# Batch 2's first-layer weights fetched ahead of layer 0's adapters, and those adapters handled behind layer A of batch 1

## The reference

```python
# layer 0
c0 = einsum('bsi,boi->bso', x, L0_cond_weight[ids0])          # one of 8 weights per batch: "W0 of batch b"
y  = einsum('bsd,od->bso', c0, L0_ffn_weight) + bias          # "W1"
lo = (c0 @ A[adapter].T) @ B[adapter].T                       # layer 0's adapters, rank 16, some batches without
x  = x + y + lo
# layer 1
c1 = x @ W2.T + b2 + scale[ids1] * ((x @ a[ids1].T) @ b[ids1].T)   # layer 1's adapters, rank 16
H  = c1 @ W3.T + b3
z  = c1 @ A3                                                  # rank 32
# softmax gates over 8 experts from H[:, odd tokens, :8] and z, scaled by their global maxima
x  = x + (H + (z * p_mix) @ Bmat * scaling)
```

## Time and profile before

| what | us |
|---|---|
| median of three runs | 122.72 (122.25 to 123.53) |
| the profiled execution | 123.07 |
| its span on the core | 121.3 |
| TensorE busy in it | 115.5 |
| VectorE, ScalarE, GpSimd busy | 84.4, 58.4, 24.0 |

### The profile page before, as it was taken

How to read it: one execution, slowest core, us unless ns; L and a number is a source line. 1 busy time by engine, 2 the same in 40 slices (tenths; PEclk the granted TensorE clock), 3 DMA queues, 4 the chain that set the end, 5 groups by cost and what they waited for, 6 DMA issues and landing times.

```text
span 121.3 us, 1920 instructions
## 1 busy us (share of the span) xinstructions
PE 115.5 (95%) x694; PEld 98.1 (81%) x694; DVE 84.4 (70%) x177; ACT 58.4 (48%) x102; POOL 24.0 (20%) x32
## 2 busy tenths in 40 slices
PE   6999999997979999999999999999999999999991
PEld 2578878885869898998989989699988587688890
DVE  0599898955797979869798443949966676503741
ACT  4389398737969393896466243160560110230000
POOL 4076873060606333300014000000000000000000
PEclk9999999999999999999999999999999999999999
DMA  3999999968995899999294000000000000000872
GB/s 101 413 419 288 331 424 312 365 213 273 266 359 174 262 246 304 286 287 249 56 337 180 0 0 0 0 5 0 0 0 0 5 0 0 0 0 3 329 276 86
DMA packets 7864, 20.78 MB, mean 171 GB/s; under 512 B 1200, under 2 KB 1584, under 8 KB 7856
## 3 DMA queue, kind: packets, MB, share of 16 engines
q1 hardware_dynamic: 4944, 10.87, 26.9%
q0 software_dynamic: 2624, 9.44, 24.1%
q10 hardware_dynamic: 288, 0.36, 0.8%
HBM read 16.39 MB, written 2.10 MB: 152 GB/s over the span
## 4 chain that ended last, share of the span: by engine, by line
PE 66%; DMA 10%; POOL 7%; DVE 6%; issue 5%; ACT 3%; ACTq 0%
PE bank L883 60%; DMA w_in<-in_W,rows_i 8%; POOL w_in L347 4%; DMA w_in<-in_W 3%; PE bank L920 2%; PE bank L1082 1%; ACT a L429 1%; POOL s_c L368 1%; DVE c_lo L564 1%; DVE w_lo L719 1%; POOL x_in L367 1%; POOL x_in L363 1%; DVE x_in L610 1%; PE bank L1153 1%; PE bank L1072 1%
## 5 line engine op out<-in xcount | busy, mean ns | idle before, releaser
L557 DVE TENSOR_TENSOR w_lo<-w_in,w_hi 128x1024 fp32r<-128x1024 f32 x16 | 19.5, 1238 | 5.2 <-ACT w_hi L394 4.5
L347 POOL DMA_INDIRECT w_in<-in_W,rows_i x16 | 17.4, 1087 | 25.7 <-DVE w_lo L557 14.9
L394 ACT CAST w_hi<-w_in 128x1024 fp32r<-128x1024 f32 x16 | 16.4, 1050 | 5.6 <-DMA w_in<-in_W,rows_i 5.6
L883 PE MATMUL bank<-c_hi,w_hi 128*128 128x256 f32 x64 | 18.2, 284 | 0.0
L883 PE MATMUL bank<-c_lo,w_hi 128*128 128x256 f32 x64 | 18.1, 283 | 0.0
L883 PE MATMUL bank<-c_hi,w_lo 128*128 128x256 f32 x64 | 18.1, 283 | 0.0
L883 PE MATMUL bank<-w_hi,x_hi 128*128 128x512 f32 x32 | 13.3, 417 | 0.7 <-DVE w_lo L557 0.7
L883 PE MATMUL bank<-m_hi,x_hi 128*128 128x512 f32 (+1 forms) x36 | 13.9, 386 | 0.0
L883 PE MATMUL bank<-m_hi,x_lo 128*128 128x512 f32 (+1 forms) x36 | 13.2, 368 | 0.0
L883 PE MATMUL bank<-m_lo,x_hi 128*128 128x512 f32 (+1 forms) x36 | 13.2, 366 | 0.0
L883 PE MATMUL bank<-w_hi,x_lo 128*128 128x512 f32 x32 | 12.6, 393 | 0.0
(11 more groups left out here) (184 smaller groups left out, 235.9 us busy)
## 6 DMA issues: line engine op xcount, KB each, us to landing
w_in<-in_W SPq DMA_DIRECT2D x5, 512.0 KB, 5.3
x_in<-in_x SPq DMA_DIRECT2D x4, 512.0 KB, 4.8
out_dram<-w_in SPq DMA_DIRECT2D x7, 256.0 KB, 2.3
be<-late_t SPq DMA_DIRECT2D x16, 69.0 KB
b<-low_t SPq DMA_DIRECT2D x16, 64.0 KB
w_in<-in_W SPq DMA_DIRECT2D x1, 1024.0 KB, 5.9
late_t<-in_late SPq DMA_DIRECT2D x1, 552.0 KB, 3.7
w_in<-in_W ACTq DMA_DIRECT2D x1, 256.0 KB, 3.5
```

Source lines behind the costliest of these rows:

```text
L347: nc.gpsimd.indirect_dma_start(w_in[:, slot, half * h:half * (h + 1)], None, W0, row).then_inc(w_landed[b][h], 16)
L394: nc.scalar.copy(part(w_hi[:, b % 2], h), raw(b, h)).then_inc(w_hi_done, 1)
L557: nc.vector.tensor_tensor(part(w_lo[:, b % 2], h), raw(b, h), f32(part(w_hi[:, b % 2], h)), ALU.subtract).then_inc(w_lo_done, 1)
L883: ins = mm(o, st, mv, start=start and n == 0, stop=stop and n == len(parts) - 1)
```

## The change

GpSimd issues both halves of W0 of batch 2 before the gather of layer 0's adapters and the scales. ScalarE's and VectorE's splits of the adapters' second half go behind their splits of W0 of batch 2. TensorE turns the adapters' first half behind layer A of batch 1 instead of ahead of it.

```diff
@@ GpSimd
             load_w(1)
+            load_w(2)
             pool.wait_ge(adapters_done, 2)
             row0 = bass.IndirectOffsetOnAxis(ap=adapter_i[:, 0:1], axis=0)
             nc.gpsimd.indirect_dma_start(rows0, None, g0, row0).then_inc(g0_landed, 16)
             nc.gpsimd.indirect_dma_start(s_c[:], None, scale, row1).then_inc(s_landed, 16)
-            load_w(2)
             for b in range(3, NB):
@@ ScalarE
             w_high(1)
-            act.wait_ge(g0_landed, 16)
-            nc.scalar.copy(b0_parts[:, 0], rows0[:, D:2 * D]).then_inc(b0_hi_done, 1)
             save_c0(0)
             act.wait_ge(ae_summed, 1)
...
             w_high(2)
+            act.wait_ge(g0_landed, 16)
+            nc.scalar.copy(b0_parts[:, 0], rows0[:, D:2 * D]).then_inc(b0_hi_done, 1)
             act.wait_ge(be_ready, 1)
@@ VectorE
             w_low(1, (1,))
-            dve.wait_ge(b0_hi_done, 1)
-            nc.vector.tensor_tensor(b0_parts[:, 1], rows0[:, D:2 * D], f32(b0_parts[:, 0]),
-                                    ALU.subtract).then_inc(b0_done, 1)
             dve.wait_ge(ae_hi_done, 1)
...
             w_low(2)
+            dve.wait_ge(b0_hi_done, 1)
+            nc.vector.tensor_tensor(b0_parts[:, 1], rows0[:, D:2 * D], f32(b0_parts[:, 0]),
+                                    ALU.subtract).then_inc(b0_done, 1)
             dve.wait_ge(be_hi_done, 1)
@@ TensorE
             product(bank[4][:], parts).then_inc(be_ready, 1)
+            layer_a(1)
             pe.wait_ge(g0_landed, 16)
             turn_rows(bank[6], rows0[:, 0:D]).then_inc(a0_ready, 1)
-            layer_a(1)
             turn_c0(0)
```

## The result

The changed kernel is slower: 128.88 us in the median (128.21 to 130.09), against 122.50 for the kernel before in the same comparison, a ratio of 1.051 with a 95% interval of 1.045 to 1.057. The span went from 121.3 to 126.7 us. The medians are 6.4 us apart and the two traces 5.4; the microsecond between these is the spread of single executions. The 5.4 us lie in three places. I read them from where TensorE starts each piece.

What follows compares the result with a forecast made beforehand. GpSimd's issues and late landing of batch 2's weights bound the kernel, leaving TensorE holes of 0.96 and 0.91 us. Removing 0.96 and about 0.45 gains 1.4, taking the median from 122.72 to 121.3 us, range 120.7 to 122.9.

Steps and rivals of the forecast that it cites:

- Order of issue: On GpSimd: four issues swap places in unchanged slots, batch 2's halves at 14.40 and 15.77, adapters 17.42, scales 18.67.
- Batch 2's halves: Weights for layer A of batch 2: second half lands no later than 25.26, so TensorE's 0.96 us hole goes.
- The adapters: Gather now behind 1 MB in GpSimd's queue: bandwidth decides, landing near where batch 2's second half did, 24.6 to 28.5.
- L: Landing time of the adapters, taken as 26.9 us with bounds 24.6 and 28.5.
- rival A: Adapters land late, L from 27.5 to 28.5: gain only 0.8 down to -0.2 us, time 122.3; chance 0.26.
- the microsecond that I took off for the spreads: L was put one microsecond before the earlier last landing, because SyncE's first spreads no longer share that DMA tail.
- The rule for what hangs on L: ScalarE and VectorE's 5.88 us pass before layer B starts at max(28.3, L + 1.6) instead of 29.93; gain 1.43 us.
- The estimate of 3.2 us: Adapters' 512 KB transfer by the skill's figures: landing near 21.6, gain the full 1.6 us; set aside for the trace.
- SyncE, the step that failed: Eight spreads start 3.7 us later, near 28.3; first four out at 31, wanted by layer B at 34.5, 3.5 left.
- rival C: SyncE's queue reaches the path: x of pair 2 lands late, layer A of batch 4 waits, up to 124.3; chance 0.08.
- a sign to look for: Sign of a wrong prediction: a hole on TensorE before layer B that ends with a spread of b.
- the half each: Packet-by-packet turns give x in SyncE's queue half of each DMA engine beside GpSimd's gathers, speaking against rival C.

Runs made afterwards that it cites:

- keep_warm: The changed kernel with 18 extra matmuls of 512 columns, results thrown away, on TensorE in its wait for pair 0's spreads; 126.45 us.
- late_b0: The changed kernel with layer B using the spreads behind 24 matmuls instead of 12 in each half, x of pair 2 still behind all eight spreads; 123.75 us.
- hold_w3: The changed kernel, but GpSimd waits for pair 0's four spreads to land before it fetches batch 3's weights; 126.28 us.
- engines_only: The changed kernel with GpSimd's issue order of before, so that only the splits and the turn are moved; 127.78 us.
- hold_w4: The changed kernel, but GpSimd fetches batch 4's weights only after pair 0's four spreads have landed; 126.37 us.
- after_again: The changed kernel run once more with no edit; 128.64 us, ratio 1.044 to the kernel before.

## Why the prediction was wrong

*Order of issue: right.* The slots are those of the earlier trace rows within 0.3 us (14.43, 15.80, 17.71, 18.95).

*Batch 2's halves: right.* ScalarE cast both in one go from 24.10, and layer A of batch 2 had no hole.

*The adapters: right in kind, too early.* I took L = 26.9 and gave 24.6 to 28.5. It was 27.60, and 27.59 to 28.77 in the traces of the seven further runs with the new issue order. The last transfer of the stretch ended near where the last one had ended before (27.9): rival A had the landing and its price right, and the microsecond that I took off for the spreads was not there. That 27.60 and 27.9 agree so well is in part luck: in the traces of the five further runs with the adapters ahead of batch 2, its second half was there for ScalarE between 26.78 and 29.51. The rule for what hangs on L held to 0.02 us: first spread at L + 1.41 = 29.01 (measured 29.02), split of turned c0 at L + 1.6 = 29.2 (measured 29.18), low-rank product earlier by 29.93 - 29.18 = 0.75 (measured 34.73 - 33.98 = 0.75). With that alone the kernel would have been 0.6% faster, not 1.2%. The estimate of 3.2 us, worked out in the prediction by the Trainium skill (*DMA: Bandwidth & Descriptors*, "Anatomy of one DMA"), stood against 9.87 here.

*SyncE, the step that failed.* It was this sentence: the first four spreads "are wanted by layer B at 34.5, [...] the 3.5 that are left should do for 64 KB each, as 4.8 do for 512 KB". They took 8.1 us from the last of them. Pair 0's spreads had no row of their own landing, and I bounded them by one fetch of x instead of from both sides by the nearest rows. The 9.24 us of the earlier trace rows, which I did use for x in rival C, would have put them at 31 + 9.2 = 40.2, close to the measured 39.0, and would have made them the rival with the highest price. I named their wait only as a sign to look for. Two things moved against each other: the spreads went 4.5 us later, and the gathers of batch 4, which the change sets free earlier, went 2.2 us forward and on top of them. I counted the second for x alone.

*The clock: not in the prediction at all.* The wait of 3.98 us on TensorE was paid 1.5 times: 3.98 for itself, 2.12 for the half clock behind it. keep_warm shows that as a cost of its own. In late_b0 a wait of 1.55 us did not bring it; in hold_w3 one of 2.02 did, and in engines_only the clock fell behind two of 2.27 and 1.42. So a short wait is not free of it, and no run here was made to find the limit.

*Rival C* (x of pair 2) had the right queue and the wrong transfer. x did land late, at 41.17 instead of my 38.6, but layer B's wait covered it here. hold_w4 shows it at work, with 0.66 us on TensorE ahead of layer A of batch 4; in late_b0 ScalarE idled 3.29 us for x and TensorE did not wait.

The size of the loss is accounted for: 128.9 with everything, 126.45 with the clock kept up, 123.2 with the spreads used later and x first. The 0.6% of gain that L left is not seen in that last kernel, but lies inside its interval (0.993 to 1.004). Why the spreads are so slow among gathers is argued, not shown. The Trainium skill (*DMA: Bandwidth & Descriptors*, "Queues, rings and completion order") has each engine take a packet from each queue in turn. If one gather half is one or a few packets per engine, four spreads take turns with four gather halves; the traces fit that (2.0 us with no half beside them, 3.0 with two partly done, 6.6 with four). In the changed kernel batch 4's second half landed at 38.8 and the last spread of pair 0 right behind it, at 39.0; and from 31 to 37 us GpSimd's queue moved 1.26 MB and SyncE's 0.23, which is far, in bytes, from the half each that I had worked out from that rule for x. But no run varied the size of the gathers' pieces.

## What to carry to other kernels

Before you move a large transfer ahead of a small one, follow the small one to its last consumer, every DMA in between included, and price each at the slowest landing that the stretch shows (9.24 us here), not at a quick one (4.8). A gather that comes free earlier through your own gain competes with those transfers at once. Where TensorE would wait for microseconds, put independent matmuls of the same product ahead of the wait: in late_b0 that left 1.55 us of the wait and kept the clock.

## What the runs showed of the hardware that was not expected

* The same 64 KB transfer from SBUF to SBUF landed 2.0 us after issue in the median with no gather beside it (hold_w3) and 6.6 with four of 512 KB (the changed kernel), 8.6 at worst (after_again).
* In the changed kernel the granted clock fell to 0.50 at about 37.2, when TensorE had stood still since 35.2, and rose to 1.00 at about 44.1, when it had been busy since 39.1.
* In engines_only it fell at 37.1 while TensorE was at work, behind waits of 2.27 and 1.42 us, the longer of which had ended at 31.93.
* GpSimd's issue of a gather took 1.95 us at 25.33, while VectorE ran two of its 1024-column subtractions (25.25 to 27.61), instead of the 0.94 that it mostly takes.
